# A graph-attention stage that scores on ScalarE, masks from SBUF on VectorE and takes the exponential on the way out of PSUM

## What is computed

```python
h = jnp.einsum('bnd,ade->bane', feat_in, W)
th = jnp.tanh(h)
attn = th @ w_src + swapaxes(th @ w_dst, 2, 3)
attn = jnp.where(attn >= 0, attn, 0.2 * attn)
attn = jnp.where(mask, -999.0, attn)
attn = jax.nn.softmax(attn, axis=-1)
feat_out = elu(einsum('banm,bame->bane', attn, h) + b)
gate = jax.nn.sigmoid(feat_in @ H_w.T + H_b)
return gate * feat_out + (1.0 - gate) * feat_in
```

## Time and profile before

| what | value |
|---|---|
| median of 3 runs | 2708.63 us (2702.85 to 2709.47) |
| the profiled execution | 2709.26 us, span 2707.5 us |
| busy share of the span, PE / DVE / ACT / POOL | 98% / 89% / 87% / 67% |
| granted TensorE clock over the span | 0.995 |
| graph stage | about the first 830 us of the span |
| DMA, mean over the span | 185 GB/s; 28 to 40 GB/s in the graph stage |

### The profile page before, as it was taken

The page is one execution under the profiler, slowest core; times in us unless marked ns, Lnnn a source line. Parts: engine busy times, 40 slices in busy tenths (PEclk is TensorE's granted clock), DMA queues, the critical chain, the costliest instruction groups (busy, mean ns, idle before and its releaser), DMA issues. The chain is left out here.

```text
span 2707.5 us, 66704 instructions
## 1 busy us (share of the span) xinstructions
PE 2640.9 (98%) x20128; PEld 2385.9 (88%) x20128; DVE 2417.2 (89%) x7209; ACT 2346.9 (87%) x6600; POOL 1804.9 (67%) x1550
## 2 busy tenths in 40 slices
PE   8999999999998999999999999999999999999996
PEld 7888888888887999999999999899999999999995
DVE  6998998898887999999999999899999999999995
ACT  7999999999998888888888888888888888888884
POOL 3777766766765677766666677766666666667665
PEclk9999999999999999999999999999999999999998
DMA  3011111111104888887778888878778887878775
GB/s 99 28 38 40 33 34 39 33 33 39 37 29 130 256 260 259 263 253 252 247 252 255 256 262 264 252 255 251 253 242 259 256 250 254 253 245 257 250 249 176
DMA packets 386754, 500.42 MB, mean 185 GB/s; under 512 B 58464, under 2 KB 349152, under 8 KB 386272
## 3 DMA queue, kind: packets, MB, share of 16 engines
q1 hardware_dynamic: 386400, 496.16, 58.2%
HBM read 219.24 MB, written 201.33 MB: 155 GB/s over the span
## 5 line engine op out<-in xcount | busy, mean ns | idle before, releaser
L794 ACT ACTIVATE probs<-logits,nmax 128x256 f32<-128x256 f32 x1152 | 571.8, 500 | 104.5 <-DVE turned_sb L1072 99.6
L570 POOL TENSOR_TENSOR probs<-probs,recs 128x1024 f32<-128x1024 f32 x288 | 545.9, 1896 | 107.8 <-DVE recs L1064 107.6
L1072 DVE STREAM_TRANSPOSE turned_sb<-probs 128x512 f32<-128x512 f32 x576 | 610.7, 1103 | 4.0 <-POOL probs L570 4.0
L1051 DVE CUSTOM_DVE_ANT_0 logits<-s,mask 128x256 f32<-128x256 f32 x1152 | 430.8, 420 | 84.1 <-PE s L1456 81.4
L548 POOL TENSOR_TENSOR residual<-x,br 128x384 f32<-128x384 f32 x192 | 191.0, 1017 | 455.9 <-DVE mix L1083 455.8
L787 ACT ACTIVATE stack<-split 64x768 fp32r<-64x768 f32 x576 | 484.8, 842 | 3.4
L76 PE MATMUL pj<-xt_hi,w_lo 128*128 128x256 f32 x1728 | 481.9, 279 | 0.8 <-DVE xt_lo L1036 0.8
L78 PE MATMUL pj<-xt_hi,w_hi 128*128 128x256 f32 x1728 | 481.0, 278 | 0.0
L77 PE MATMUL pj<-xt_lo,w_hi 128*128 128x256 f32 x1728 | 480.8, 278 | 0.0
L665 ACT ACTIVATE g_exps<-g_v,g_nmax 128x256 f32<-128x256 f32 x768 | 385.3, 515 | 3.0 <-DVE g_nmax L961 0.7
L779 ACT ACTIVATE split<-pj,bc 128x256 fp32r<-128x256 f32 x576 | 239.6, 467 | 163.2 <-PE pj L78 107.3
(11 more groups left out here) (118 smaller groups left out, 7401.3 us busy)
## 6 DMA issues: line engine op xcount, KB each, us to landing
turned<-turned_sb SPq DMA_DIRECT2D x288, 512.0 KB, 5.0
pt_copy<-turned SPq DMA_DIRECT2D x288, 512.0 KB, 4.6
stack<-split SPq DMA_DIRECT2D x576, 128.0 KB, 4.4
y<-out SPq DMA_DIRECT2D x128, 384.0 KB, 5.2
x<-y SPq DMA_DIRECT2D x96, 384.0 KB, 3.1
x<-x SPq DMA_DIRECT2D x32, 384.0 KB, 3.0
adj<-adj SPq DMA_DIRECT2D x128, 64.0 KB, 3.1
w_whole<-att_w SPq DMA_DIRECT2D x24, 192.0 KB, 2.9
```

The costliest lines, as they stand in the source:

```text
L570: pool.tensor_tensor(probs[:, heads, :, :].rearrange("p h t n -> p (h t) n"), probs[:, heads, :, :].rearrange("p h t n -> p (h t) n"), rec ...
L794: last = act.activation(probs[:, (HEADS * u + h) % 4, t, :], logits[:, h % 2, t, :], ACT.Exp, scale=-1.0, bias=nmax[:, u, h, t:t + 1], acc ...
L1051: last = dve.tensor_tensor_reduce(out=logits[:, h % 2, t, :], in0=s_ps[h % 2][:, t, :], in1=mask[u][:, t, :], scale=-HEAD_DIM ** -0.5, sca ...
L1072: last = dve.transpose(turned_sb[b][:, :, :].rearrange("p k (z h q) -> p k z h q", z=NT, h=2 * NT)[:, :, kt], probs[:, 2 * b:2 * b + 2, :, ...
```

## The change

The graph stage is written anew on all engines; the attention stage is left as it is.

- The source and target terms (`g_rows_of_sd`) are written to DRAM as 12 rows and read back by three DMAs that copy them onto all 128 partitions (`g_lay_rows`, `g_spread`); VectorE turns the source terms into columns (`g_turn_rows`).
- The scores are no product any more. ScalarE makes them from SBUF: `Prelu` of minus the spread targets plus the source term as bias (`g_leaky`), two instructions of 128x256 for each head.
- `g_maximum` reads these scores from SBUF and the mask, now an fp32 tile, from SBUF too.
- The maximum is subtracted by VectorE for the even heads and by GpSimd for the odd ones (`g_subtract`), six heads each. GpSimd's six instructions that built the right-hand sides are gone.
- TensorE turns the shifted scores, and ScalarE takes the exponential while it copies them out of PSUM, one instruction of 128x512 for each head (`g_exp`); there are no other copies of them out of PSUM.
- The row sums are taken by TensorE with columns of ones (`g_sums_of_four`), turned back beside the contexts and inverted from PSUM (`g_copy_sums`, `g_invert_sums`).
- The source and target product is made in plain fp32, and the tanh state is copied once and not split.
- A sample's end moves one slot further back (`old`), and eight buffers hold scores where three held them.

```diff
-        g_mask = [sb(f"g_mask{p}", [P, NT, N], F32R) for p in range(2)]
+        g_mask = [sb(f"g_mask{p}", [P, NT, N]) for p in range(2)]
...
+            def g_lay_rows(half, u):
+
+                held(sp, g_rows_ready, at(1, half, u, 1), passed)
+                sp.dma_start(targets_dram[u], g_rows[g_TARGETS, :]).then_inc(g_rows_laid, 16)
+
+            def g_spread(half, u, i):
+
+                sp.wait_ge(g_rows_laid, 16 * (2 * half + u + 1))
+                held(sp, g_leaky_done, earlier(GAT_HEADS, half, u, -GAT_HEADS), passed)
+                heads = slice(i * GAT_HEADS // g_PARTS, (i + 1) * GAT_HEADS // g_PARTS)
+                sp.dma_start(g_targets[u][:, heads, :], targets_dram[u, heads, :].rearrange("h n -> (h n)").partition_broadcast(P).rearrange("p (h n) -> p h n", n=N)).then_inc(g_targets_spread[u][i], 16)
...
+            def g_subtract(half, u, h):
+
+                v = g_v_of(u, h)
+                pool.wait_ge(g_maxed, at(GAT_HEADS, half, u, h + 1))
+                pool.tensor_tensor(v, v, g_nmax[:, u, h, :].unsqueeze(2).to_broadcast([P, NT, N]), ALU.subtract).then_inc(g_odd_shifted, 1)
...
+            def g_leaky(half, u, h):
+                g_targets_ready(act, half, u, h)
+                for t in range(NT):
+                    last = act.activation(g_v_of(u, h)[:, t, :], g_targets[u][:, h, :], ACT.Prelu, scale=-1.0,
+                                          bias=g_source[u][:, t, h:h + 1], alpha=LEAKY)
+                last.then_inc(g_leaky_done, 1)
...
             def g_exp(half, u, h):
-                act.wait_ge(g_maxed, at(GAT_HEADS, half, u, h + 1))
-                act.wait_ge(g_transposed, at(GAT_HEADS // 2, half, u, h // 2 - 1))
-                for t in range(NT):
-                    last = act.activation(g_exps[:, h % 4, t, :], g_v_sb[:, h % 3, t, :], ACT.Exp, scale=-1.0,
-                                          bias=g_nmax[:, u, h, t:t + 1], accum_out=g_sums[:, u, h, t:t + 1])
-                last.then_inc(g_exped, 1)
+
+                act.wait_ge(g_transposed, at(GAT_HEADS, half, u, h + 1))
+                act.wait_ge(g_contexts, at(g_GROUPS, half, u, h // g_QUAD - 1))
+                act.activation(g_pt_sb[:, g_pt_slot(u, h)], pt_ps[h % 2][:, :, :], ACT.Exp, scale=-1.0).then_inc(g_exped, 1)
...
             def g_maximum(half, u, h):
-                held(dve, g_lrelu, at(GAT_HEADS, half, u, h + 1), passed)
+                v = g_v_of(u, h)
+                dve.wait_ge(g_mask_ready, at(1, half, u, 1))
+                held(dve, g_leaky_done, at(GAT_HEADS, half, u, h + 1), passed)
                 for t in range(NT):
                     last = dve.tensor_tensor_reduce(
-                        out=g_v_sb[:, h % 3, t, :], in0=s_ps[h % 2][:, t, :], in1=g_v_sb[:, h % 3, t, :], scale=-1.0,
+                        out=v[:, t, :], in0=v[:, t, :], in1=g_mask[u][:, t, :], scale=-1.0,
                         scalar=BIG, op0=ALU.add, op1=ALU.min, accum_out=g_nmax[:, u, h, t:t + 1])
                 last.then_inc(g_maxed, 1)
...
+            def g_subtract(half, u, h):
+
+                v = g_v_of(u, h)
+                dve.wait_ge(g_maxed, at(GAT_HEADS, half, u, h + 1))
+                for t in range(NT):
+                    last = dve.tensor_scalar(v[:, t, :], v[:, t, :], g_nmax[:, u, h, t:t + 1], None, ALU.subtract)
+                last.then_inc(g_even_shifted, 1)
...
+            def g_sums_of_four(u, g):
+
+                ones = g_sel[:, 1 + g * GAT_DIM:1 + (g + 1) * GAT_DIM]
+                for kt in range(NT):
+                    for i in range(g_QUAD):
+                        pe.matmul(s_ps[1][i * GAT_DIM:(i + 1) * GAT_DIM, 0, :], ones, g_pt_sb[:, g_pt_slot(u, g * g_QUAD + i), kt, :],
+                                         start=g == 0 and kt == 0, stop=g == g_GROUPS - 1 and kt == NT - 1)
```

More of the change, by code:

```diff
@@ L41, in f32, with g_every_slot, sample @@
     return ap.bitcast(F32)
[L44 to L50, removed]
+def g_every_slot(slot):
+    def sample(k):
+        return divmod(k, 2) if 0 <= k < B else None
+    for k in range(B):
+        slot(sample(k + 1), sample(k), sample(k - 1), sample(k - 2), sample(k - 3), sample(k - 4))
 def every_slot_of_all_layers(slot, behind=3):
@@ L1191, in _ @@
-            g_lo_of_step(0, 0, g_X)
-            g_lo_of_step(0, 0, g_X + 1)
+            g_split_x(*first, 0)
+            g_split_x(*first, 1)
             dve.wait_ge(g_w_hi_done, 1)
             dve.tensor_tensor(g_w_lo[:, 0], g_w_stage[:, 0], f32(g_w_hi[:, 0]), ALU.subtract).then_inc(g_w_split, 1)
-            dve.wait_ge(g_ident_loaded, 16)
-            dve.tensor_copy(g_ident_r[:, :], ident[:, :])
-            for p in range(2):
-                for part, rows in ((g_z_left, g_DST), (g_s_dst, g_SRC)):
-                    last = dve.tensor_scalar(part[p][rows, :], ident[rows, 0:1].to_broadcast([g_HALF, N]), 0.0, 1.0, ALU.mult, ALU.add)
@@ L1269, in g_make_back @@
                 if t == 0:
                     pe.wait_ge(g_ctx_read, at(g_GROUPS, half, u, g_GROUPS))
-                    pe.wait_ge(g_gate_done, at(NT, *(cur or (half, u)), NT))
-                if nxt and t == 1:
-                    pe.wait_ge(g_pj_hi, at(len(g_HI_STEPS), *nxt, g_HI_STEPS[g_H]))
-                if not nxt:
-                    pe.wait_ge(g_back_read, at(NT, half, u, 0))
-                for g in range(g_GROUPS):
+                    pe.wait_ge(g_sums_read, at(1, half, u, 1))
@@ L1583 @@
     w_sd = np.zeros((D, P), np.float32)
+    groups = GAT_HEADS * GAT_DIM // P
+    sel = np.zeros((P, 1 + groups * GAT_DIM), np.float32)
+    sel[:, 0] = 1.0
+    for g in range(groups):
+        sel[:, 1 + g * GAT_DIM + g] = 1.0
     for h in range(GAT_HEADS):
         rows = slice(h * GAT_DIM, (h + 1) * GAT_DIM)
[L1586 to L1589 removed]
         for q in range(4):
[L1591 removed]
+            source, target = 32 * q + h, 32 * q + GAT_HEADS + h
+            w_sd[rows, source], w_sd[rows, target] = a["L0_gnn_w_src"][h, :, 0], a["L0_gnn_w_dst"][h, :, 0]
+            sel[target, 0] = -1.0
     names = [f"L{layer}_gnn_" for layer in range(1, LAYERS + 1)]
```

923 lines of the change are left out of this document (456 added, 467 removed).

## The result

| what | before | changed |
|---|---|---|
| median of 4 runs each | 2706.35 us (2702.85 to 2709.47) | 3008.8 us (3003.76 to 3012.94) |
| ratio | | 1.112, 95% interval 1.109 to 1.114 |
| profiled execution | span 2707.5 us | 3008.63 us, span 3006.5 us |
| granted TensorE clock over the span | 0.995 | 0.952 |
| period of a sample, 200 to 800 us | 25.2 us | 34.9 us |

The change made the kernel 302 us slower. The direction had been given 0.85; the size, 2894 us with 2980 as the upper end, was too small: **the prediction was wrong**. All of the difference lies in the graph stage, and it is the period: 9.7 us more for each of 31 samples is 301 us. (Periods in this text: VectorE reads 24 maxima out per sample, so the readouts between 200 and 800 us, divided by 24, are the samples in those 600 us. Before: 571, thus 23.8 samples. After: 412, thus 17.2 samples.

The account below looks back on a forecast made before the run. VectorE, its work plus holding by GpSimd on a shared SBUF path, was taken to bound the changed graph stage. 2709.3 + 31 x 5.4 + 13 + 5 = 2894.7, thus 2894 us; range 2775 to 2980.

Parts of the forecast that it names:

- They are not independent: Graph stage: GpSimd instructions and VectorE ones with two SBUF inputs, or fast SBUF-to-SBUF ones, exclude each other nearly their whole time.
- Rival 1: Graph stage: engines stay independent, so TensorE bounds at 22.4 us a sample and the kernel takes 2634 us; chance 0.10.
- VectorE's work, 19.6: VectorE in the graph stage: 22.6 us a sample before, less 6.5 removed, plus 3.5 added, gives 19.6 us.
- VectorE is therefore held for 13.3 us less: GpSimd holds the path 13.3 us a sample; about 2.5 of it falls beside VectorE's unlocked work, so doesn't hold VectorE.
- the rule: Each GpSimd instruction holds the shared path for its duration less 0.20 us: 17.3 - 20 x 0.20 = 13.3 a sample.
- Period: 19.6 + 13.3 - 2.5 = 30.4 us: Graph stage period: VectorE's work plus GpSimd's holding less their overlap, 5.4 us more than before; bounds 26.5 and about 33.
- Rival 4: TensorE, idle a quarter of the time, falls to its lower clock in the graph stage; 2980 us and up, chance 0.03.
- Rival 3: VectorE's maximum runs at half rate, 6.5 us more a sample, period 37, 3097 us; chance 0.06.
- Rival 2: Graph stage: the lock exists but the lists interleave well, period 24.5 to 26.3 us, 2712 to 2768 at the slower end; chance 0.09.
- The small terms: Period before 25.0 us; 5 us for the first sample's DRAM row write and spread; 13 us for twelve weight splits.
- 16 samples take 480 to 490 us: Sign that the forecast is right: time for 16 samples of the graph stage, against 400 us before.
- PE and ScalarE fall to about seven tenths: Sign that the forecast is right: busy shares of TensorE and ScalarE in the graph stage, both waiting for VectorE.

Follow-up runs that it names:

- e1: The changed kernel, but VectorE copies the mask once per sample into a PSUM tile, where the 24 maxima read it; 2877.3 us.
- e2: The changed kernel with the split of the second half moved ahead of maxima 0 to 2 in VectorE's list, nothing else; 2859.5 us.
- e5: The changed kernel with 56 products, never read, on TensorE ahead of the projection that waits; 2963.0 us.
- e4: The changed kernel with each of GpSimd's six subtractions cut to 2 of its 512 columns; 2903.0 us.
- e6: The changed kernel with mask in PSUM, early split, x's high parts cast by ScalarE and the second low part behind maximum 0; 2778.5 us.

## Why the prediction was wrong, point by point

- **"They are not independent": right.** The instances spread from 0.404 to 2.05 us, and e1 turns them all back to 0.41 by moving one operand to PSUM. The Trainium skill (SBUF — State Buffer, section "SBUF: two separate sides") states that lock; the runs agree, for the custom maximum too, but not for GpSimd's layer norm, inside which maxima run. Rival 1 had been given 0.10 because the maximum had never been seen with two SBUF inputs; it falls.
- **VectorE's work, 19.6: nearly right,** 20.2 measured. A free subtraction has a pitch of 0.26 where 0.21 was put, which is 0.6 over twelve of them.
- **"VectorE is therefore held for 13.3 us less" 2.5: near in size, partly by luck.** 10.8 us forecast, 9.3 held (5.8 and 3.5, without the clamp). Two errors stand in it. GpSimd has 16 instructions a sample and not 20; with 16 the rule gives 17.3 - 3.2 = 14.1, the period 31.2 and the time 2919 us, still far below the result. And the rule itself, duration less 0.20, fits `mix`, `residual`, the bias and the subtractions (they let go 0.13 to 0.15 us before their end), but not the layer norm, which the rule charges with 2.9 us and which holds the maxima for 0.1 and VectorE's subtractions for 0.2.
- **"Period: 19.6 + 13.3 - 2.5 = 30.4 us": the step that failed.** It sums what VectorE does and is held for, and so puts VectorE's idleness at nothing, without a reason. It is 5.0 us a sample, and the period 34.9. The prediction looked at which engine is fullest and at the lock, and never asked what stands behind a held instruction in VectorE's list. The answer was in the order of instructions: the split for the next sample, behind three maxima, with a whole projection of TensorE waiting. That PE and ScalarE "wait for VectorE" was written down as slack without a price; the chain comes back to VectorE through the transposes, the exponential and the scores. e2 shows it: the pair moved, nothing else, the idleness is 1.1 and the period 30.1. In the timeline above 7.2 us pass from the start of maximum 0 to the split, where free instructions would need 2.6; the maxima are held for 3.8 of them and the subtractions for 0.8.
- **Rival 4, the lower clock, 0.03: wrong as it was put.** It was priced as a separate misfortune that needs TensorE to become the bound. It came as part of the same loop: TensorE idles 8 us in one piece, and then works through the projection at the lower level. Here the granted clock is 0.87 in the stretch (1.00 in the earlier trace rows). The time, 3008.8, lies where this rival had put it (2980 and up), and its sign, a clock under 1.0, came true; but its price is 1.7 us a sample and 46 us in all (e5), and the rest of the excess is not the clock.
- **Rival 3, half rate: refuted.** The Trainium skill (Vector Engine (DVE) Microarchitecture Reference, section "Points that are easy to get wrong") gives half throughput for a scalar-tensor-tensor with two fp32 inputs in SBUF; carried over to the maximum, that would have doubled it. The shortest of the maximum's 312 instances shown above is 0.404 us, the same as with PSUM. The gate's scalar-tensor-tensor (line 975), of just that form, takes 0.948 us for 768 columns, where a 384-wide instruction with an input in PSUM takes 0.56; the runs don't agree with the Trainium skill here.
- **Rival 2, good interleaving: not reached by the order as it was.** It had two things right: the lists decide, and the layer norm (line 520 before, line 529 now) hardly holds the path. But the layer norm is a small part of the sum. With the split moved and the mask in PSUM the period is 26.0.
- **The small terms.** The period of before is 25.2 and not 25.0. ScalarE starts on the first scores at 27.55 us, after 27.13 in the kernel before, and no 5 us were lost. A split of weights makes a sample 1.7 us longer (35.8 instead of 34.1), where 1.1 was put, 20 us in all instead of 13; it is part of the measured 34.9. With the periods as measured the sum closes: 2709.3 + 31 x 9.7 = 3010, measured 3008.8; for e2 2709.3 + 31 x 4.9 = 2861, measured 2859.5.
- **"16 samples take 480 to 490 us": 558.** "PE and ScalarE fall to about seven tenths": 0.69 and 0.59. VectorE's busy share was to be over nine tenths and is 0.86, and this was the first sign that something beside the lock was at work.

What stays open: how much of the wait the lock makes and how much the order alone. The runs have the late split with the whole lock (changed) and with a part of it (e1, e4), and TensorE waits in each; no run has the late split with no lock at all, and none takes the lock off the three heads ahead of it alone.

## What to carry to other kernels

Where an operand of VectorE moves from PSUM to SBUF, sum the holding by GpSimd on top of the work, and then look at each held instruction for what stands behind it in its engine's list: a short producer that another engine needs for a long step belongs ahead of the instructions that can be held. A sum of busy times gives the period only if no list waits; before trusting it, follow one chain from engine to engine until it comes back, and price the wait with the clock that TensorE shows after such a gap. A mask that 24 instructions of a sample read cost one copy of 0.69 us to lay into PSUM; the engine that has room should make it.

## What the runs showed of the hardware

- The wait for the shared path is inside the record of the held instruction: 0.42 us becomes 2.02, with no idle time before it. A group's mean against its shortest instance is the view that shows it (0.657 against 0.404).
- GpSimd's instructions differ in how they hold the path. Under `mix` (1.82 us) or `residual` (1.85) a maximum waits until 0.13 to 0.14 us before the end; inside the layer norm's instructions (1.66 us each) 34 maxima ran from start to end at a mean of 0.46 (77 in e2, at 0.56). Why is not shown.
- After 8.1 us of idleness TensorE runs nine 384-wide products, 3 us, at a granted clock of 0.50, and is at its full level for the next ones (records of 0.34 again at 531.76). In e6 the same products are at the lower level after 2.5 us of idleness (records of 0.52). In e2, where the projection waits 0.94, its products have 0.34.
- Filler products that nobody reads made the kernel 46 us faster.
- `Prelu` with a pointer for its bias runs at the exponential's duration: four of 128x256 in 1.69 us at 529.50, thus 0.50 each and 0.40 from start to start, as forecast from the earlier trace rows.
